# Eight fetch buffers instead of two in the last stage of a two-layer graph/expert kernel

## The reference, cut to what matters

```python
def _L1_ffn_ref(x, Wg, bg, W1, b1, W2, b2):
    ...
    top_w, top_i = jax.lax.top_k(gate_logits, TOP_K)
    top_w = jax.nn.softmax(top_w, axis=-1)
    w_dense = jnp.sum(jax.nn.one_hot(top_i, E, dtype=xf.dtype) * top_w[..., None], axis=1)
    out = jnp.zeros_like(xf)
    for e in range(E):
        h = jax.nn.gelu(xf @ W1[e] + b1[e], approximate=False)
        out = out + w_dense[:, e:e + 1] * (h @ W2[e] + b2[e])
    return out.reshape(B, L, D)
...
x = x + _L1_ffn_ref(_layernorm(x, axis=-1), ...)
return x
```

## Time and profile before

| what | value |
|---|---|
| median of 3 runs | 1738.74 us (1738.03 to 1741.6) |
| the profiled execution: its time | 1740.67 us |
| the profiled execution: span from first to last instruction | 1738.7 us |
| last POOL scatter of the expert stage starts | 1669.14 us |
| first fetch of the last stage is issued | 1676.37 us |
| busy over the span: PE / DVE / ACT / POOL | 74% / 59% / 43% / 47% |
| DMA traffic over the span | 168.57 MB, mean 97 GB/s |

### The profile page before, as it was taken

The page is one execution under the profiler, slowest core; times in us unless marked ns, Lnnn a source line. Parts: engine busy times, 40 slices in busy tenths (PEclk is TensorE's granted clock), DMA queues, the critical chain, the costliest instruction groups (busy, mean ns, idle before and its releaser), DMA issues. The chain is left out here.

```text
span 1738.7 us, 34925 instructions
## 1 busy us (share of the span) xinstructions
PE 1287.0 (74%) x8909; PEld 1090.6 (63%) x8909; DVE 1017.5 (59%) x3818; ACT 740.3 (43%) x1710; POOL 812.2 (47%) x839
## 2 busy tenths in 40 slices
PE   3988888837677777349999995767773299999930
PEld 2777666726566667238888884545552189888920
DVE  1788888757767776335555553888885122222236
ACT  2555555515655555214444441443432155555510
POOL 3255555561455554614444443277676144445420
PEclk9999999968989988669999997888876599999975
DMA  6100000000000000145656563122211366766647
GB/s 157 23 1 0 0 0 0 1 1 1 20 28 28 25 25 27 40 133 190 201 189 199 191 201 105 55 71 73 71 36 41 104 214 219 218 217 220 218 133 203
DMA packets 134763, 168.57 MB, mean 97 GB/s; under 512 B 17584, under 2 KB 105520, under 8 KB 134704
## 3 DMA queue, kind: packets, MB, share of 16 engines
q1 hardware_dynamic: 98224, 122.49, 23.6%
q0 software_dynamic: 17408, 35.95, 5.9%
q10 hardware_dynamic: 19072, 9.46, 1.9%
HBM read 123.47 MB, written 44.37 MB: 97 GB/s over the span
## 5 line engine op out<-in xcount | busy, mean ns | idle before, releaser
L1602 POOL DMA_INDIRECT rows<-m_yb,m_dsti x288 | 276.6, 960 | 361.1 <-DVE m_dsti L1734 312.5
L1627 PE MATMUL psum<-m_xT,m_w 128*128 128x256 f32 (+1 forms) x864 | 200.2, 381 | 1.3 <-ACT m_xT L1668 1.3
L964 POOL DMA_INDIRECT dispatch<-a_flat,a1r_pos x128 | 129.9, 1015 | 111.4 <-DVE a1r_pos L945 69.4
L964 POOL DMA_INDIRECT dispatch<-g_flat,g1r_pos x128 | 133.2, 1041 | 74.3 <-DVE g1r_pos L945 37.3
L1627 PEld LDWEIGHTS psum<-m_xT,m_w 128*128 128x128 f32 (+1 forms) x864 | 149.1, 179 | 28.9 <-ACT m_xT L1668 1.9
L1701 DVE TENSOR_TENSOR m_yb<-psum,m_w 128x256 f32<-128x256 f32 x72 | 30.6, 425 | 218.6 <-PE psum L1642 218.6
L1683 ACT ACTIVATE m_sg<-psum,m_w 128x256 f32<-128x256 f32 x288 | 117.9, 471 | 92.4 <-PE psum L1632 91.3
L1632 PE MATMUL psum<-m_xT,m_w 128*128 128x256 f32 x576 | 141.2, 389 | 7.4 <-ACT m_xT L1666 7.4
L1642 PE MATMUL psum<-m_w,m_sg 128*128 128x128 f32 x1152 | 140.5, 275 | 0.6 <-DVE m_yb L1701 0.6
L1676 ACT ACTIVATE m_sg<-psum 128x256 f32<-128x256 f32 (+1 forms) x216 | 78.8, 382 | 142.9 <-PE psum L1627 98.5
L1717 DVE TENSOR_TENSOR m_hT<-psum,m_sg 128x256 f32<-128x256 f32 (+1 forms) x216 | 88.4, 422 | 83.7 <-ACT m_sg L1676 81.1
(11 more groups left out here) (250 smaller groups left out, 2971.2 us busy)
## 6 DMA issues: line engine op xcount, KB each, us to landing
m_w<-in_c_wall SPq DMA_DIRECT2D x72, 578.0 KB, 3.6
m_w<-in_c_wall SPq DMA_DIRECT2D x72, 533.0 KB, 3.4
m_xg<-dispatch SPq DMA_DIRECT2D x144, 130.0 KB, 3.5
g1c_y<-rows SPq DMA_DIRECT2D x32, 256.0 KB
fin_y<-rows ACTq DMA_DIRECT2D x32, 256.0 KB, 3.5
rows<-m_yb,m_dsti POOLq DMA_INDIRECT x288, 3.1
out<-x SPq DMA_DIRECT2D x16, 256.0 KB, 3.0
dispatch<-nobody SPq DMA_DIRECT2D x24, 130.0 KB, 6.8
```

What stands on the lines that cost most here:

```text
L964: pool.indirect_dma_start(out=dest, out_offset=bass.IndirectOffsetOnAxis(ap=self.pos[:, k, p:p + 1], axis=0), in_=flat[:, p, :], in_offset ...
L1602: pool.indirect_dma_start(out=rows_out, out_offset=bass.IndirectOffsetOnAxis(ap=dsti[j][:, t:t + 1], axis=0), in_=yb[j][:, t, :], in_offse ...
L1627: i = pe.matmul(bank[0:cn, TILE * m:TILE * m + TILE], w[j][:, HID * m + c0:HID * m + c0 + cn], xT[j % 2][:, :], start=(m == 0), stop=True, ...
```

## The change

`Combine` gets a parameter for the number of buffers. phase_gnn1 keeps two. phase_finish asks for eight (DEPTH): eight buffers of 4 KB per partition, each with its own `landed` semaphore. ACT issues the 16 fetches of groups 0 to 7 in straight-line code without a wait, and then in one turn of a loop those of groups 8 to 15, each after group g - 8 has been mixed. DVE's loop handles eight groups in each of two turns instead of two groups in each of eight. The stores and the 8 instructions of a group are the same.

```diff
+DEPTH = 8
...
-    def __init__(self, ctx, nc, name, state, rows):
-        self.state = state
+    def __init__(self, ctx, nc, name, state, rows, depth=2):
+        self.state, self.depth = state, depth
...
-        self.ys = [ctx.enter_context(nc.sbuf_tensor(f"{name}_y{i}", [128, 2, PG, C], F32)) for i in range(2)]
-        self.landed = [take_semaphore(ctx, nc, f"{name}_landed{i}") for i in range(2)]
+        self.ys = [ctx.enter_context(nc.sbuf_tensor(f"{name}_y{i}", [128, 2, PG, C], F32)) for i in range(depth)]
+        self.landed = [take_semaphore(ctx, nc, f"{name}_landed{i}") for i in range(depth)]
...
-        for b in range(2):
-            g = turn * 2 + b
-            eng.wait_ge(*self.mixed.before(g, turns=2))
+        for b in range(self.depth):
+            g = turn * self.depth + b
+            if not isinstance(turn, int) or turn > 0:
+                eng.wait_ge(*self.mixed.before(g, turns=self.depth))
             eng.sem_inc(self.gate, 1)
             for k in range(2):
                 eng.dma_start(self.ys[b][:, k, :, :], self.rows[:, k, bass.ds(g * PG, PG), :]).then_inc(self.landed[b], 16)
...
-        dve.wait_ge(self.landed[b], (g - b) * 16 + 32)
+        dve.wait_ge(self.landed[b], (g - b) * (32 // self.depth) + 32)
...
-        M = Combine(ctx, nc, "fin", state, rows)
+        M = Combine(ctx, nc, "fin", state, rows, depth=DEPTH)
...
-                turns(act, 0, GROUPS // 2, lambda turn: M.fetch(act, turn))
+                M.fetch(act, 0)
+                turns(act, 1, GROUPS // DEPTH, lambda turn: M.fetch(act, turn))
...
-                turns(dve, 0, GROUPS // 2, lambda turn: [M.vector_mix(dve, turn * 2 + b, b, x) for b in range(2)])
+                turns(dve, 0, GROUPS // DEPTH, lambda turn: [M.vector_mix(dve, turn * DEPTH + b, b, x) for b in range(DEPTH)])
```

## The result

The changed kernel took 1723.72 us (median of 4 runs, 1720.72 to 1724.62) beside 1740.17 us for the kernel before (4 runs). The ratio is 0.9901, with a 95% interval of 0.988 to 0.9923: 1.0% faster, 16.5 us between the medians. Predicted were 1722.8 us and a gain of 15.9 us. The profiled execution took 1724.6 us, with a span of 1722.6 us.

What follows compares the result with a forecast made beforehand. The last stage was taken to be bound by the two-buffer ring, neither DVE nor the DMA engines. 16.6 us of waits removed less 0.7 us given back made 15.9 us, median 1738.74 to 1722.8 us, range 1720.8 to 1728.8.

Steps and rivals of the forecast that it cites:

- The ring: Last stage: 2.45 us of mixing + 4.83 us of fetching = 7.28 us per two groups with two buffers.
- 16.6 us of waits go: Last stage: DVE's 13 waits for fetched rows after the entry, 16.6 us in all, removed by more buffers.
- DVE's pace, 2.43 us per group: Last stage: DVE mixes a group in 2.43 us where no fetch is awaited; sixteen groups take 38.9 us.
- The other way, 36.4 + 2.4 us: Check of DVE's time in the last stage: 36.4 us busy plus 2.4 us of gaps gives 38.8 us.
- The DMA engines at 305 GB/s, 0.7 us given back: Last stage: 2.58 us per group near 305 GB/s; DVE waits 0.4 us, rounded up to 0.7 us.
- the lead: Last stage: fetches, alone until the first store, are 1.6 us ahead of DVE by group 2.
- The entry stays: DVE's entry into the last stage, a 13.4 us wait, is kept; the first group starts at 1680.40 us.
- ACT, addresses, code at nothing: Last stage: ACT's issuing, DVE's register operations (one per instruction) and the longer loop body were each to cost nothing.
- one sign: Profile after, last stage: ACT issues 16 fetches in a row from 1676.4 us on, within some 10 us.
- The tail of 2.9 us: From DVE's end to the end of the span, unchanged at 1738.7 - 1735.8 = 2.9 us.
- the DMA engines as the pace: Rival, last stage: DMA engines set the pace; 1724.1 us at 290 GB/s, 1728.2 at 260; chance 0.31.
- The collapse under a full queue: Rival, last stage: mixed traffic falls to 157 GB/s, 21 us slower, 1760 us; all slower cases together 0.03.

Runs made afterwards that it cites:

- two, three and four groups in the ring: Fetch of group g waits for g - 2 (kernel before), g - 3 (unrolled, eight buffers) or g - 4 (four buffers): last stage 62.3, 47.7 and 44.8 us.
- the old wait: Changed kernel with eight buffers and unrolled bodies, but each fetch waits for the group two before: 1742.33 us, ratio 1.001, last stage 64.5 us.
- the half-mixing run of the kernel before: Kernel before with DVE's second four instructions of each group left out, all DMAs kept: last stage 52.5 us, ratio 0.9943.
- four profiles of three kernels: Unrolled code waiting for the group two before: eight buffers (64.5 us twice), two buffers (64.7 us), three semaphore increments between a group's fetches (64.3 us).

## Why the prediction was right, step by step

- **The ring.** Shown from three sides: the stage length over two, three and four groups in the ring; the gain lost with the old wait although everything else stayed; and the half-mixing run of the kernel before, 52.5 us where the ring gave 52. The prediction says that group g - 8 has been mixed 8 x 2.43 = 19 us before group g is due; it is seven groups, 17 us, and nothing hangs on it.
- **16.6 us of waits go.** They went, but for 0.28 us at the second group.
- **DVE's pace, 2.43 us per group.** Mis-sized: 2.34 us measured. The prediction read it from group 2 to group 3 and took group 3 for one that needn't wait. By the trace the second fetch of group 3 landed at 1690.02 (issued at 1686.06), and DVE began 0.24 us later, just as it began at 1697.54 after the landing of 1693.55 + 3.75 = 1697.30 in the earlier trace rows. So this start was held by the fetch too, although the views list no wait there. A group that really needn't wait starts while the last instruction of the group before is still at work, which saves 0.09 us: eight instructions across such a border take 2.19 us, two fours 2 x 1.14 = 2.28. The other way, 36.4 + 2.4 us, has the same fault: in the kernel before, 14 of the 15 borders lack this overlap. The window of the stage shows it, 35.25 us busy instead of 36.38 for the same 128 instructions, 1.1 us less (and a DMA share of 0.95 where the earlier trace rows had 0.72):

```profile
1676.00:1722.60 46.60, 0.00 (x0) 0.00 (x0) 35.25 (x128) 0.00 (x0) 0.00 (x0) 0.50 0.95 271
```

The same 2.34 us could have been read before, from the second half of group 0 to that of group 1, the only border of the whole stage without a wait:

```profile
1681.69 2.19 DVE L1784 SCALAR_TENSOR_TENSOR x<-fin_y,w,x 128x128 f32 x8 [0.15 <-DVE x L1784]
...
1684.03 1.14 DVE L1784 SCALAR_TENSOR_TENSOR x<-fin_y,w,x 128x128 f32 x4 [0.15 <-DVE x L1784]
```

- **The DMA engines at 305 GB/s, 0.7 us given back.** Mis-sized, on the careful side: 327 to 338 GB/s with fetches and stores mixed from 1688 us on, 0.3 us given back. Up to 1684 us, though, they were slower than the 302 GB/s assumed (216 GB/s with the start-up in it, then 269 GB/s), and that is where the one wait lies. So the lead ran the other way round than in the prediction. It was to be 1.6 us at group 2 and to be used up, at 2.58 us per group against 2.43; by the trace the last fetch of group 2 landed 0.8 us before DVE began with it, that of group 15 2.6 us before. In between a group's fetches landed every (1714.72 - 1686.05) / 13 = 2.21 us, and DVE took 2.34. The Trainium skill (DMA: Bandwidth & Descriptors, Measured) gives 425 GB/s for a load of 16 MB issued from GpSimd. No 4 us of the last stage came near it in any run here, some 344 GB/s at the most; elsewhere in the changed kernel, while an expert stage loads its weights, the single microsecond from 762.25 us on reached 414 GB/s (the one from 762.00 on 333).
- **The entry stays.** It was 4.39 us instead of 4.03, the spread of executions (4.03 to 4.48 over the two kernels' four profiles).
- **ACT, addresses, code at nothing.** Nothing here cost time, but one sign was missed. The first 16 fetches were to be issued within some 10 us; the first line below has them from 1677.4 to 1690.0, 12.6 us, at up to 1.52 us each. From the eighth on ACT was held up, at a full queue as it seems, and nobody waited for it. The register operations stayed at one per instruction:

```profile
L1775 ACTq DMA_DIRECT2D fin_y<-rows x16: 383/732/1522, 1677.4 to 1690.0; - x16
...
L1786 DVEq FUSED_REGOPS  x128: 57/79/110, 1681.6 to 1718.9; - x128
```

No wait for its own issue appears on DVE in the stage, and where the loop turns, behind group 7, the pace is 2.37 us instead of 2.34. The Trainium skill (Runtime: NRT & Kernel Launch, Instruction fetch mechanics) has a taken branch wait for a fetch when its target lies outside the two held blocks; the trace agrees in that the one backward jump of this body of some 150 instructions cost 0.03 us at most, and no run here tried a longer one. That this speaks against long unrolled bodies was the prediction's own conclusion; the section says that kernels prefer full unrolling where they can.
- **The tail of 2.9 us.** 1722.6 - 1719.75 = 2.85 us. The last fetch is issued at 1707.7 us and lands 7.1 us later, at 1714.7, well before DVE's end: the last store meets nearly empty engines (a DMA share of 0.44 from 1716 us on), although most stores took 5.9 us.

The stage came out 17.1 us shorter instead of 15.9: 1.1 us is DVE's pace, 0.4 us the smaller wait, less 0.4 us of the longer entry; 0.1 us is the tail and rounding. That the time came within 1 us is in part luck. The two mis-sized terms make 1.5 us more gain; the longer entry (0.4 us) and the median of the kernel before, which came out at 1740.17 us and not at 1738.74, worked the other way. Of the rivals, the DMA engines as the pace were nearest: they are level with DVE, 2.30 to 2.34 us. The collapse under a full queue did not come: where the engines are full the rate was 316 and 322 GB/s before, 325 to 339 with four buffers and 327 to 338 with eight, in windows of 4 us.

## What to carry to other kernels

When an engine and its transfers both show 60 to 80% busy and the transfers pause, look for a ring: work on a buffer, free it, fetch, land. Its length divided by the number of buffers is the pace, and the buffers that it takes are those that bring this under the pace of the slowest engine: here 7.06 us over 2.34 us says three. But the ring grows when more is under way: with three groups in it a round took 7.6 us, still more than 3 x 2.34 = 7.0, and 2.9 us of the stage were left; four were as good as eight. Beyond that, the next bound has to be priced from rows where the engines run unbroken, and here two of them, DVE and the DMA engines, lay within 0.04 us per group of each other.

## What was not expected

- The same fetches and stores under the same waits took 2 us longer in the last stage when ACT's and DVE's loops were unrolled over eight groups (64.3 to 64.7 us in four profiles of three kernels, 62.3 and 62.8 in two of the kernel before). Neither the place of the buffers nor the spacing of the two fetches explains it; the order of store and fetch differs, and was not tried alone.
- The DMA engines moved more with fetches and stores mixed than with fetches alone: 327 to 342 GB/s in windows of 4 us once both queues were filled, against 287 to 302 GB/s, both in pieces of 512 bytes.
- The median time to landing of a fetch went from 3.5 to 6.3 us while the stage became 27% shorter: with queued transfers it measures the queue, not the transfer.
